# A graph-network layer on one core: every row gather gets a wait of its own

## The reference, cut to what matters

```python
h = jnp.maximum(_layernorm(x), 0.0)
deg = jnp.maximum(jnp.zeros((n,)).at[dst].add(1.0), 1.0)
edge_weight = (deg[src] * deg[dst]) ** (-0.5)
edge_msg = relu(edge_attr @ W1e + b1e) @ W2e + b2e
messages = (h[src] + edge_msg) * edge_weight[:, None]
agg = segment_sum(messages, dst, n)
combined = (1.0 + gin_eps) * h + agg
out = relu(combined @ W1n + b1n) @ W2n + b2n + h
out = out * rsqrt(mean(out * out) + RMS_EPS) * rms_w
result = x + out
```

## Time and profile before

| | |
|---|---|
| median of 3 runs | 1485.35 us (1485.29 to 1486.96) |
| the profiled execution's own time | 1484.08 us |
| its span, first to last instruction | 1482.4 us |
| its mean granted PE clock | 0.961 of full speed |
| busy time of PE, DVE, ACT, POOL | 1109.6, 954.0, 695.3, 833.3 us |
| gathers on POOL | 802, 789.6 us busy |

### The profile page before, as it was taken

The page is one execution under the profiler, slowest core; times in us unless marked ns, Lnnn a source line. Parts: engine busy times, 40 slices in busy tenths (PEclk is TensorE's granted clock), DMA queues, the critical chain, the costliest instruction groups (busy, mean ns, idle before and its releaser), DMA issues. The chain is left out here.

```text
span 1482.4 us, 34585 instructions
## 1 busy us (share of the span) xinstructions
PE 1109.6 (75%) x12030; PEld 777.2 (52%) x12030; DVE 954.0 (64%) x4416; ACT 695.3 (47%) x1295; POOL 833.3 (56%) x846
## 2 busy tenths in 40 slices
PE   0528777877887788778777877787788778877966
PEld 0415555555555555555555555555555555555643
DVE  6986666665666666666666666566557656666628
ACT  7645444444444444444444444444444444444615
POOL 1165665565566555565565656566556655666325
PEclk9998999999999999999999999999999999999989
DMA  5153333333333333333333333333333333333144
GB/s 171 44 168 96 88 101 91 93 91 93 91 92 103 82 91 93 101 94 82 92 101 94 84 90 101 91 94 92 92 90 94 87 97 92 95 100 76 40 184 165
DMA packets 67529, 145.16 MB, mean 98 GB/s; under 512 B 24275, under 2 KB 25862, under 8 KB 67232
## 3 DMA queue, kind: packets, MB, share of 16 engines
q1 hardware_dynamic: 40688, 86.72, 19.1%
q0 software_dynamic: 25664, 53.02, 15.5%
q10 hardware_dynamic: 1008, 3.21, 0.6%
HBM read 136.31 MB, written 6.57 MB: 96 GB/s over the span
## 5 line engine op out<-in xcount | busy, mean ns | idle before, releaser
L978 POOL DMA_INDIRECT arena<-node_rows,idx x802 | 789.6, 985 | 529.2 <-remote 217.9
L1130 ACT ACTIVATE arena<-bank 128x512 f32<-128x512 f32 (+1 forms) x450 | 244.4, 553 | 503.5 <-remote 319.1
L1138 ACT ACTIVATE arena<-bank 128x686 f16<-128x686 f32 x405 | 366.1, 904 | 212.6 <-remote 158.2
L1204 DVE SCALAR_TENSOR_TENSOR arena<-iota_h,hi_f,bank 128x98 f32<-128x98 f32 x810 | 223.5, 313 | 310.0 <-remote 168.6
L1059 PE MATMUL bank<-t_words,arena 128*126 128x256 f16 x2205 | 303.6, 279 | 0.4 <-ACT arena L1138 0.4
L1003 PE MATMUL bank<-w1e,arena 64*128 64x128 f32 x3240 | 261.7, 283 | 0.0
L1048 PE MATMUL bank<-arena 128*128 128x343 f16 x810 | 188.6, 315 | 89.3 <-DVE arena L1188 86.8
L997 PE MATMUL bank<-bias_split,ones_bf 64*128 64x256 bf16 x810 | 118.3, 287 | 177.6 <-ACT arena L1130 98.6
L1059 PEld LDWEIGHTS bank<-t_words,arena 128*126 128x126 f16 x2205 | 240.9, 140 | 2.4 <-ACT arena L1138 0.7
L1188 DVE TENSOR_SCALAR arena<-iota_c,code 128x343 f16<-128x343 f16 x810 | 230.8, 328 | 4.1 <-PE bank L1048 4.0
L1003 PEld LDWEIGHTS bank<-w1e,arena 64*128 64x128 f32 x3240 | 229.1, 199 | 0.0
(11 more groups left out here) (196 smaller groups left out, 873.9 us busy)
## 6 DMA issues: line engine op xcount, KB each, us to landing
arena<-in_attr SPq DMA_DIRECT2D x135, 384.0 KB
arena<-low_src SPq DMA_DIRECT2D x47, 288.0 KB, 3.6
arena<-node_rows,idx POOLq DMA_INDIRECT x802
node_rows<-arena SPq DMA_DIRECT2D x1, 3160.5 KB, 8.9
arena<-in_x ACTq DMA_DIRECT2D x7, 448.0 KB, 10.8
arena<-node_rows SPq DMA_DIRECT2D x6, 516.0 KB, 10.3
t_words<-s_kp SPq DMA_DIRECT2D x6, 512.0 KB, 9.7
arena<-in_x SPq DMA_DIRECT2D x6, 512.0 KB, 12.8
```

Of the source, the lines that this page charges most:

```text
L978: nc.gpsimd.indirect_dma_start(out=edge_rows[:, u, j, 0:ROW], out_offset=None, in_=table, in_offset=bass.IndirectOffsetOnAxis(ap=idx[:, u, ...
L1130: ins = nc.scalar.activation(out.rearrange("p (j o) d -> p o j d", o=2), of, ACT.Relu)
L1138: nc.scalar.activation(strip[:, u, :, 2 * p * W:2 * p * W + 2 * W].rearrange("p k (t w) -> p t k w", t=2), pair_bank[:, :].rearrange("p (t ...
L1204: ins = nc.vector.scalar_tensor_tensor(out=loop.picked[:, j * LK:(j + 1) * LK], in0=iota_h[:, :], scalar=hi_f[:, column(c), at_slot], in1= ...
```

## The change

The odd gathers get a wait too: for `pair_ps`, the count product, with the same number as the even gather beside it waits for in `z_ps`.

```diff
                     for j in fetched(c, i):
-                        if j % 2 == 0 and c > 0:
-                            pool.wait_ge(z_ps, (c - 1) * U + (j // 2 + 5))
+                        if c > 0:
+                            pool.wait_ge(pair_ps if j % 2 else z_ps, (c - 1) * U + (j // 2 + 5))
                         nc.gpsimd.indirect_dma_start(
```

## The result

The changed kernel takes 1443.86 us (median of 4 runs, 1442.77 to 1444.38), the kernel before 1485.94 in the same set of runs: a ratio of 0.9715, interval 0.9698 to 0.9732. It is 2.9% faster, where no change was forecast and the range ended at 1481.5. The span is 1441.0 us, and the mean granted clock of PE is 0.991 in place of 0.961.

A forecast was written before the change was run, and what follows sets the result against it. The prediction took the loop of PE and ACT handing work to and fro to set the time. It summed 1484.08 + 0 + 0 + 0 = 1484.1, forecasting a median of 1485.4 us, range 1481.5 to 1490.

The forecast's parts named there:

- A fulfilled wait costs nothing: POOL, 392 gathers with an added wait: already fulfilled waits cost 0; upper bound 118 us, within 529.2 us of idle time.
- Slot 1's odd gather is the one that moves: POOL, slot 1: the odd gather waits for the late count product and starts at 722.70, 2.27 us later.
- Slot 3 unchanged: POOL, slot 3: even gather starts as before, odd one at 729.14 in place of 729.07, unchanged within 0.1 us.
- Readers of the rows and SP's loads see no difference: Queued behind the moved gathers: rows read some 29 us later, SP waits for an unmoved last gather; on the path 0.
- Contention with DVE costs nothing on the path: DVE, slot 2: the moved gather costs 9 to 18 us in 44 steps, covered by a margin of 1.6 us; 0.
- Rival B: Slower by contention: the moved gather delays DVE in slot 2 and the 1.6 us margin isn't real; 1494.6 us, chance 0.14.
- On the path: 0: Whole kernel: added waits, what queues behind the gathers and DVE contention each add 0 to the profiled 1484.08 us.
- Why the signal is so late the profile doesn't show: Slot 1's count product signal: on record at 718.64, ACT and DVE start at 722.46; every step, 3.7 us each, cause left open.
- Rival C: The clock, pause of slots 1 and 2: two drops fewer give 1482.3 us, two more 1488.5; 1.57 us each; chance 0.10.
- Rival D: Faster by relief, slot 2: even gather no longer beside line 1188, up to 0.1 us a step, 1481.4 us; chance 0.08.

The follow-up runs named there:

- the second set: Changed kernel, slot 1's odd gather left out, all gathers left out, and fills for odd gathers, run in turn with the kernel before, which took about 1442 us.
- the third: Set of four kernels with other waits or gathers left out, against the kernel before at 1183.9 us: 1183.32, 1183.13, 1147.01, 1184.08.

## Why the prediction was wrong

- *A fulfilled wait costs nothing*: right. The eight waits other than slot 1's make 1.0011.
- *Slot 1's odd gather is the one that moves*: right in place. It moved by less than the 2.27 us forecast: 3.20 us behind the relu of its slot (702.05 - 698.85) against 2.35 before (720.43 - 718.08), because the signal it waits for came 1.4 us earlier. "Slot 3 unchanged" held (0.24 and 1.49 us behind the relu of that slot in both traces); in slot 2 the odd gather stood at its own wait (0.74 us idle), which was forecast to be past.
- *Readers of the rows and SP's loads see no difference*: nothing in the runs speaks against it.
- *Contention with DVE costs nothing on the path*: no cost of it shows, and a few tenths of a microsecond a step can't be told apart beside the gain. The gather took 1.15 us in place of 0.94, line 1188 324 ns in the mean against 328. Rival B, slower, did not come: slot 1's wait alone makes the kernel faster. B also took PE's starts for modelled; it is the ends that are.
- *"On the path: 0", the sum*: wrong, and this is the step that failed. It rested on "Why the signal is so late the profile doesn't show" and went on as if the lateness of 3.8 us were PE's own. It depends on the gathers: without the odd one in slot 1 it goes down by 1.4 us, with only every other slot's gathers the signals of the slots between are prompt, without odd gathers nearly all are. The forecast looked only at who waits for the moved gather; the effect was on a signal of PE, which waits for no gather there.
- *Rival C, "Nothing in the change touches PE's wait itself, so this is weak"*: the same mistake. It had the right place (the drops behind the pause) and the right price a step (1.57 us in two single steps, 1.27 in the mean of 41), but a count of two steps where 24 of 41 changed.
- *Rival D, faster by relief*: the right direction by luck. It expected up to 4 us from slot 2, and slot 2 became 1.1 us longer a step.

There was a sign in the trace of before. In five slots of nine ACT was idle for "remote" (the relus of slots 0, 6, 7 and 8 and the copy of slot 1), a releaser that this view names when no instruction of a plausible end is found; the last step, in which few gathers are left, has slots of mostly 2.2 to 2.7 us where the steps before have 3.15. Neither was followed up.

**What stays open.** What holds PE's signals was not found. Shown are: where it occurs, it takes a second gather close behind a first (single ones don't do it, at nine a step, and a fill behind a gather doesn't either); 1.4 to 1.5 us between their starts in place of 1.25 don't help; the signals then come in a bunch, mostly 1.6 to 1.7 us after the start of the last gather, that of slot 1's count product 2.0 us after it (722.46 - 720.43); and it was there in the first measurement and in three of five sets, and absent in two. That it is the signals and not PE's work that is late shows in the semaphore events that the trace holds beside the instructions: in the kernel before, the edge product, the count product and the gathered sum of one slot end on record at 714.79, 715.33 and 715.89, and their signals are logged at 716.43, 716.51 and 716.57. Of all signals of the edge and count products and the gathered sums a third are less than 0.2 us apart, where PE's records of them end at least 0.5 us apart but for 1% or so; with even gathers alone it is 1%.

One chip had it in the second set and not in the third, so it isn't a fixed trait of a chip. Whether a later start of slot 1's gather alone would bring more, where the hold exists, isn't known: both runs of that kernel fell into sets without it, and the run with all odd gathers behind the copy, the only one of the kind with the hold, was slower than the changed kernel.

That the clock's drops hang on the pause's length is read from the traces: in the kernel before (two traces) and the one without slot 1's wait, 62 of the 99 steps with a pause of 2.1 to 2.2 us have a drop, and none of the 24 with a shorter one, nor any of the 164 steps of the changed kernel (three traces) and of slot 1's wait alone. No run changed the pause by itself, and why 37 steps with the long pause keep their clock isn't shown. In the run behind the copy the clock also drops behind pauses in other slots.

## What to carry to other kernels

When the profile shows an engine starting over 1 us after the record of the instruction that it waits for has ended, and the releaser is "remote", find out what else is under way at that time before taking any wait as given: here a run without half of the gathers would have shown a fifth of the time. An edit whose own delays all lie in idle time can still shorten a pause of PE (here 2.2 to 0.8 us), and with it take drops of the clock away. And a pacing wait should be judged against the kernel before in the same set of runs: the same pair of kernels is 1.3 to 2.9% apart where the signals are held, and other waits of this kind made at most 0.3% where they aren't.

## What the hardware showed that was not expected

PE's signals (its additions to semaphores) reached the waiting engines late and in bunches while gathers by indirect DMA were under way in twos or more, in three of five sets; that of slot 1's count product 3.8 us after the start of the product's record. Where none or single ones were, and in the two other sets, they came at once (0.05 us behind the record). In the same kernel this makes slots of 3.15 or of 2.5 us, and 1485 or 1184 us in all. A drop of the granted clock to half (1.2 of 2.4 GHz) came in 24 of the 39 steps with a PE pause of 2.2 us in slot 1 and in none where it was 0.8 us; a step with a drop was 1.27 us longer. Fills of 1.01 us on POOL lengthened a DVE instruction from 328 to 526 ns in the mean, gathers of 0.98 us didn't (328 beside 308 with no gathers at all).
